# Attention and feed-forward layer on one core: the second layer norm folded into the second weights and the last sum, four tiles sharing a bank for the input transposes and for the output products

## The reference, cut to what matters

```python
def _layernorm(x, eps=1e-5):                      # no gain, no bias
    return (x - mean(x)) / sqrt(var(x) + eps)

x = x + attention(_layernorm(x), Wq, Wk, Wv, Wp, bp)
# attention: q, k, v per head, softmax(q k / 8) v, heads joined, times Wp, plus bp
x = x + ffn(_layernorm(x), ln1_g, ln1_b, w1, b1, ln2_g, ln2_b, w2, b2)

def ffn(x):
    h = layer_norm(x, ln1_g, ln1_b)
    h = einsum('bsd,hd->bsh', h, ternary_quant(w1)) + b1
    h = gelu(h)
    h = layer_norm(h, ln2_g, ln2_b)               # over the 512 hidden columns
    return einsum('bsh,dh->bsd', h, ternary_quant(w2)) + b2
```

## Time and profile before

| | |
|---|---|
| runs | 1081.8, 1083.76, 1084.48 us, median 1083.76 us |
| the profiled execution | 1080.79 us, of which the span of the core's work is 1079.0 us |
| busy share of the span | PE 95%, PE weight loads 74%, DVE 86%, ACT 88%, POOL 85% |
| granted TensorE clock, mean | 0.989 |
| first stage | from the start to about 951 us |
| second stage alone | from about 951 us to the end |

### The profile page before, as it was taken

How to read it: one execution, slowest core, us unless ns; L and a number is a source line. 1 busy time by engine, 2 the same in 40 slices (tenths; PEclk the granted TensorE clock), 3 DMA queues, 4 the chain that set the end, 5 groups by cost and what they waited for, 6 DMA issues and landing times.

```text
span 1079.0 us, 40480 instructions
## 1 busy us (share of the span) xinstructions
PE 1021.4 (95%) x16160; PEld 801.4 (74%) x16160; DVE 923.9 (86%) x1989; ACT 952.3 (88%) x1322; POOL 920.0 (85%) x874
## 2 busy tenths in 40 slices
PE   2878999988999999999999999999999999789998
PEld 1456776766877777778777777777777778567777
DVE  5889888898888888888888888888888888579998
ACT  2677997987999999999999999999999999779997
POOL 3376997987899999999999999999999998967785
PEclk9999999999999999999999999999999999989999
DMA  9201232112222233222322222222222222311111
GB/s 201 68 12 30 42 41 40 36 33 36 42 42 42 41 42 42 41 41 40 35 44 40 40 39 40 39 40 39 42 41 42 41 42 41 61 30 32 41 32 50
DMA packets 159785, 47.56 MB, mean 44 GB/s; under 512 B 141168, under 2 KB 159344, under 8 KB 159600
## 3 DMA queue, kind: packets, MB, share of 16 engines
q1 hardware_dynamic: 159600, 44.97, 23.0%
HBM read 7.21 MB, written 4.19 MB: 11 GB/s over the span
## 4 chain that ended last, share of the span: by engine, by line
PE 74%; ACT 10%; DVE 7%; issue 6%; POOL 2%; DMA 1%; ACTq 0%; SPq 0%; DVEq 0%; POOLq 0%
PE S L471 14%; PE PV L490 7%; PE S L463 7%; PE PV L492 5%; PE PV L491 5%; PE QK L431 5%; PE QK L432 5%; PE QK L433 5%; PE M L444 5%; ACT zTh L750 3%; ACT z L737 3%; PE misc L524 2%; PE misc L504 2%; PE misc L525 2%; PE misc L526 2%
## 5 line engine op out<-in xcount | busy, mean ns | idle before, releaser
L805 POOL TENSOR_TENSOR pl<-p,ph 128x1024 f16<-128x1024 f32 x256 | 545.4, 2136 | 85.0 <-ACT ph L677 80.8
L669 ACT ACTIVATE p<-S,s_exp 128x1024 f32<-128x1024 f32 x256 | 285.3, 1114 | 56.3 <-PE S L471 53.7
L943 DVE TENSOR_REDUCE negmax<-M 128x4 f32<-128x1024 f32 x256 | 311.9, 1218 | 7.4 <-PE M L444 4.0
L677 ACT ACTIVATE ph<-p 128x1024 f16<-128x1024 f32 x256 | 270.6, 1057 | 8.1
L971 DVE TENSOR_TENSOR QKl<-QK,QKh 128x512 f16<-128x512 f32 x256 | 176.3, 689 | 98.7 <-ACT QKh L685 98.5
L490 PEld LDWEIGHTS PV<-V,ph 128*128 128x128 f16 x2048 | 185.3, 98 | 65.9 <-issue 63.9
L490 PE MATMUL PV<-V,ph 128*128 128x65 f16 x2048 | 216.3, 194 | 11.7 <-DVE O L965 11.5
L491 PE MATMUL PV<-V,ph 128*128 128x64 f16 x2048 | 214.2, 193 | 0.0
L492 PE MATMUL PV<-V,pl 128*128 128x65 f16 x2048 | 213.4, 194 | 0.0
L492 PEld LDWEIGHTS PV<-V,pl 128*128 128x128 f16 x2048 | 189.2, 97 | 0.0
L491 PEld LDWEIGHTS PV<-V,ph 128*128 128x128 f16 x2048 | 189.1, 97 | 0.0
(11 more groups left out here) (145 smaller groups left out, 2481.0 us busy)
## 6 DMA issues: line engine op xcount, KB each, us to landing
result<-X SPq DMA_DIRECT2D x16, 256.0 KB, 2.3
X<-in_L_attn_query SPq DMA_DIRECT2D x7, 512.0 KB, 7.1
OT<-O SPq DMA_TRANSPOSE x64, 4.3
O<-in_L_attn_Wq SPq DMA_DIRECT2D x1, 512.0 KB, 4.7
O<-in_L_attn_Wk SPq DMA_DIRECT2D x1, 512.0 KB, 6.5
X<-in_L_attn_query SPq DMA_DIRECT2D x2, 256.0 KB, 5.2
O<-in_L_attn_Wv SPq DMA_DIRECT2D x1, 512.0 KB, 5.9
w<-in_L_ffn_w SPq DMA_DIRECT2D x2, 256.0 KB, 5.0
```

The source lines that it names most:

```text
L669: e.activation(p32[r][:, :, :, :].rearrange("p i m n -> p (i m n)"), S[:, :], ACT.Exp, scale=s_exp[:, :]).then_inc(s_ex, 1)
L677: e.activation(ph[r][:, :, :, :].rearrange("p i m n -> p (i m n)"), p32[r][:, :, :, :].rearrange("p i m n -> p (i m n)"), ACT.Copy).then_i ...
L805: e.tensor_tensor(pl[r][:, :, :, :].rearrange("p i m n -> p (i m n)"), p32[r][:, :, :, :].rearrange("p i m n -> p (i m n)"), ph[r][:, :, : ...
L943: e.tensor_reduce(negmax[g % 2][:, :].rearrange("p (i c) -> p i c", i=2)[:, :, NB * jj:NB * jj + NB], M[:, :].rearrange("p (i t m) -> p i ...
```

## The change

Second layer norm. `z` is no longer made. PE transposes the gelu's output `a` itself. The mean is taken out of the second weights once (a new matmul with `ones` at step `MEAN2` = 56, new DVE instruction `T2_less`), since subtracting from each row of products the mean is the same as using weights whose mean over the 512 hidden rows is gone. The inverse root, times the scale factors `s_f1` and `s_f2`, goes into the last sum as `rs2`. POOL makes it for four tiles at a time. The split of the turned values now also multiplies by `inv_f1` (one number per partition): on ACT a scale operand, on DVE `scalar_tensor_tensor` in place of `tensor_tensor`.

Groups of four (`FG`). The transposes of four tiles' `y` fill one bank, and `yTh` and `yTl` are made with one instruction of 512 columns for four tiles. The products of four tiles fill one `misc` bank, and the sums of a group begin when its fourth product is done. `y` is made by ACT, with `r1` and a new `nm1` that POOL computes with two more instructions per batch. `FFN_LEAD` goes from 2 to 5, and the lags change.

```diff
-FFN_LEAD, TAIL = 2, 7
-QK_RING, P_RING, XT_RING, A_RING = 10, 4, 3, 5
+FFN_LEAD, TAIL = 5, 7
+QK_RING, P_RING, XT_RING, A_RING = 10, 4, 3, 4
+FG = 4
-L_YT, L_YLO, L_HID, L_STAT, L_NORM, L_ZT, L_ZLO, L_OUT, L_SUM = 1, 2, 3, 4, 6, 7, 8, 9, 10
+L_YT, L_HID, L_ZT, L_OUT, L_SUM = 1, 6, 7, 9, 13
-T1_SPLIT, GAINS2, BIAS2 = MAXIMA["t1"][2] + 1, 52, 56
+T1_SPLIT, GAINS2, MEAN2, T2_SPLIT, BIAS2 = MAXIMA["t1"][2] + 1, 52, 56, 58, 64
...
         def f_bank(i):
-            return misc_banks[i % 2]
+            return misc_banks[1 - i // FG % 2]
...
+                if t == MEAN2:
+                    dst = misc_take("mean2", 0)
+                    e.wait_ge(s_w, W_AT["T2"])
+                    for c in range(FC):
+                        op = e.matmul(dst[:, 0:D], ones[:, :], above[1][:, c * D:(c + 1) * D], start=c == 0, stop=c == FC - 1)
+                    op.then_inc(s_fb, 1)
...
             def f_hidden(i):
-                e.wait_ge(s_ylo, i + 1)
+                g, k = divmod(i, FG)
+                e.wait_ge(s_ylo, g + 1)
...
             def f_zT(i):
-                e.wait_ge(s_z, i + 1)
+                e.wait_ge(s_a, i + 1)
...
             def f_out(i):
+                g, k = divmod(i, FG)
                 e.wait_ge(s_zlo, i + 1)
-                if i < 2:
-                    e.wait_ge(*misc_done(*misc_lists[i][-1]))
-                if i >= 2:
-                    e.wait_ge(s_out, i - 1)
-                o = f_bank(i)[:, 0:D]
+                if k == 0 and g < 2:
+                    e.wait_ge(*misc_done(*misc_lists[1 - g][-1]))
+                elif k == 0:
+                    e.wait_ge(s_out, FG * (g - 1))
+                o = f_bank(i)[:, k * D:(k + 1) * D]
...
-            def f_norm(i):
-                k = i % A_RING
-                e.wait_ge(s_nm2, i + 1)
-                if i >= 2:
-                    e.wait_ge(s_zt, i - 1)
-                e.activation(z[i % 2][:, :], a[k][:, :], ACT.Identity, scale=r2[k][:, :], bias=nm2[k][:, :]).then_inc(s_z, 1)
+            def f_y(i):
+                g, k = divmod(i, FG)
+                e.wait_ge(s_nm1, i // NB + 1)
+                if g >= 2:
+                    e.wait_ge(s_yt, FG * (g - 2) + k + 1)
+                e.activation(y[g % 2][:, k, 0:D - 1], X[:, i, 0:D - 1], ACT.Identity, scale=r1[:, i:i + 1],
+                             bias=nm1[:, i:i + 1]).then_inc(s_y1, 1)
...
-                             ACT.Copy).then_inc(s_zhi, 1)
...
+                             ACT.Identity, scale=inv_f1[:, :]).then_inc(s_zhi, 1)
+
+            def f_yhi(g):
+                e.wait_ge(s_yt, FG * g + FG)
+                if g >= 2:
+                    e.wait_ge(s_pre, FG * (g - 1))
+                e.activation(yTh[g % 2][:, :, :], yT_bank[g % 2].rearrange("p (k n) -> p k n", k=FG),
+                             ACT.Copy).then_inc(s_yhi, 1)
...
-                for lag, fn in ((L_NORM, f_norm), (L_HID, f_gelu), (L_ZT, f_zhi), (L_YT, f_yhi)):
+                for lag, fn in ((L_HID, f_gelu), (L_ZT, f_zhi), (0, f_y)):
                     if 0 <= u - lag < NT:
                         fn(u - lag)
+                if u % FG == 0 and FG <= u <= NT:
+                    f_yhi(u // FG - 1)
...
                 e.tensor_tensor(r1[:, tl], ve1[:, tl], half[:, :], ALU.pow).then_inc(s_r1, 1)
+                e.wait_ge(s_r1, b + 1)
+                e.tensor_tensor(mr1[:, tl], mv1[:, tl, 0], r1[:, tl], ALU.mult).then_inc(s_mr1, 1)
+                e.wait_ge(s_mr1, b + 1)
+                e.tensor_scalar(nm1[:, tl], mr1[:, tl], -1.0, None, ALU.mult).then_inc(s_nm1, 1)
...
+            def f_root(g):
+                k = g % 2
+                e.wait_ge(s_mv2, FG * g + FG)
+                e.tensor_scalar(ve2[k][:, :], mv2[k][:, :, 1], EPS, None, ALU.add).then_inc(s_ve2, 1)
+                e.wait_ge(s_ve2, g + 1)
+                e.tensor_tensor(r2[k][:, :], ve2[k][:, :], half[:, 0:1].to_broadcast([P, FG]), ALU.pow).then_inc(s_r2, 1)
+                e.wait_ge(s_r2, g + 1)
+                if g >= 2:
+                    e.wait_ge(s_out, FG * (g - 1))
+                e.tensor_scalar(rs2[k][:, :], r2[k][:, :], s_f12[:, :], None, ALU.mult).then_inc(s_rs2, 1)
...
+                if t == MEAN2:
+                    e.wait_ge(s_fb, 3)
+                    weight(e.scalar_tensor_tensor(above[1][:, :].rearrange("p (c d) -> p c d", c=FC),
+                                                  misc("mean2", 0)[:, 0:D].unsqueeze(1).to_broadcast([P, FC, D]), -1.0 / F,
+                                                  above[1][:, :].rearrange("p (c d) -> p c d", c=FC), ALU.mult, ALU.add),
+                           "T2_less")
...
-                e.tensor_tensor(zTl[i % 3][:, :, :], z_bank[i % 2][:, :].rearrange("p (c n) -> p c n", c=FC),
-                                zTh[i % 3][:, :, :], ALU.subtract).then_inc(s_zlo, 1)
+                e.scalar_tensor_tensor(zTl[i % 3][:, :, :], z_bank[i % 2][:, :].rearrange("p (c n) -> p c n", c=FC),
+                                       inv_f1[:, :], zTh[i % 3][:, :, :], ALU.mult, ALU.subtract).then_inc(s_zlo, 1)
 
             def f_sum(i):
-                e.wait_ge(s_f, i + 1)
+                g, k = divmod(i, FG)
+                e.wait_ge(s_f, FG * g + FG)
                 e.wait_ge(s_xb, i + 1)
-                e.scalar_tensor_tensor(X[:, i, :], f_bank(i)[:, 0:D], s_f2[:, :], X[:, i, :],
+                e.wait_ge(s_rs2, g + 1)
+                e.scalar_tensor_tensor(X[:, i, :], f_bank(i)[:, k * D:(k + 1) * D], rs2[g % 2][:, k:k + 1], X[:, i, :],
                                        ALU.mult, ALU.add).then_inc(s_out, 1)
...
+                if u % FG == 1 and FG < u <= NT + 1:
+                    f_ylo(u // FG - 1)
+                for lag, fn in ((L_ZT, f_stats), (L_SUM, f_sum), (L_ZT, f_variance), (L_ZT, f_zlo)):
```

More of the change, by code:

```diff
@@ L206, in layer @@
         st1, mv1 = sb("st1", [P, NB, 6]), sb("mv1", [P, NT, 2])
-        ve1, r1 = sb("ve1", [P, NT]), sb("r1", [P, NT])
+        ve1, r1, mr1, nm1 = (sb(n, [P, NT]) for n in ("ve1", "r1", "mr1", "nm1"))
         setup = ExitStack()
@@ L233, in layer @@
         setup.close()
-        y = [sb(f"y{i}", [P, D]) for i in range(2)]
-        yTh = [sb(f"yTh{i}", [P, P], F16) for i in range(3)]
-        yTl = [sb(f"yTl{i}", [P, P], F16) for i in range(3)]
+        y = [sb(f"y{i}", [P, FG, D]) for i in range(2)]
+        yTh = [sb(f"yTh{i}", [P, FG, P], F16) for i in range(2)]
+        yTl = [sb(f"yTl{i}", [P, FG, P], F16) for i in range(2)]
         a = [sb(f"a{i}", [P, F]) for i in range(A_RING)]
-        z = [sb(f"z{i}", [P, F]) for i in range(2)]
         zTh = [sb(f"zTh{i}", [P, FC, P], F16) for i in range(3)]
@@ L591, in f_hidden @@
                 o = pre_bank[i % 2]
-                e.matmul(o, yTh[i % 3][:, :], T1h[:, :], start=True, stop=False)
-                e.matmul(o, yTh[i % 3][:, :], T1l[:, :], start=False, stop=False)
-                e.matmul(o, yTl[i % 3][:, :], T1h[:, :], start=False, stop=True).then_inc(s_pre, 1)
+                e.matmul(o, yTh[g % 2][:, k, :], T1h[:, :], start=True, stop=False)
+                e.matmul(o, yTh[g % 2][:, k, :], T1l[:, :], start=False, stop=False)
+                e.matmul(o, yTl[g % 2][:, k, :], T1h[:, :], start=False, stop=True).then_inc(s_pre, 1)
             def f_zT(i):
-                e.wait_ge(s_z, i + 1)
+                e.wait_ge(s_a, i + 1)
                 if i == 0:
@@ L621, in f_yT @@
             def f_yT(i):
+                g, k = divmod(i, FG)
                 e.wait_ge(s_y1, i + 1)
                 if i == 0:
+                    e.wait_ge(s_y0, 2)
                     e.wait_ge(s_mx, NP)
-                if i >= 2:
-                    e.wait_ge(s_ylo, i - 1)
-                e.transpose(yT_bank[i % 2][:, 0:P], y[i % 2][:, :], ident[:, :]).then_inc(s_yt, 1)
+                if k == 0 and g >= 2:
+                    e.wait_ge(s_ylo, g - 1)
+                e.transpose(yT_bank[g % 2][:, k * P:(k + 1) * P], y[g % 2][:, k, :], ident[:, :]).then_inc(s_yt, 1)
             e.wait_ge(s_ident, 2)
@@ L741, in f_gelu @@
                 if i >= A_RING:
-                    e.wait_ge(s_z, i - A_RING + 1)
-                    e.wait_ge(s_mv2, i - A_RING + 1)
-                e.activation(a[i % A_RING][:, :], pre_bank[i % 2][:, :], ACT.Gelu, scale=s_f1[:, :]).then_inc(s_a, 1)
+                    e.wait_ge(s_zt, i - A_RING + 1)
+                    e.wait_ge(s_st2, i - A_RING + 1)
+                e.activation(a[i % A_RING][:, :], pre_bank[i % 2], ACT.Gelu, scale=s_f1[:, :]).then_inc(s_a, 1)
             def f_zhi(i):
@@ L876, in pool_program @@
                     e.wait_ge(s_w, W_AT["ffn_weights"])
-                for lag, fn in ((L_STAT, f_root), (L_STAT, f_negmean), (0, f_bias)):
-                    if 0 <= u - lag < NT:
-                        fn(u - lag)
+                if 0 <= u < NT:
+                    f_bias(u)
+                if (u - L_ZT) % FG == FG - 1 and 0 <= u - L_ZT < NT:
+                    f_root((u - L_ZT) // FG)
```

86 lines of the change are left out of this document (31 added, 55 removed), and 1 row of the table W_AT.

## The result

The changed kernel took 1075.95 us (median of 6 runs, 1074.98 to 1079.46), the kernel before 1083.76 us (6 runs, 1081.8 to 1084.48) in the same comparison. The ratio is 0.9936, interval 0.992 to 0.9952. The profiled execution took 1075.9 us, span 1074.1. So the change is faster, as forecast, but by more than the range allowed (1077.0 to 1084.6).

The account below looks back on a forecast made before the run. The prediction took PE to bound attention and DVE, at 1.96 us a tile, the second stage. Its terms -4.25, -2.35, +2.0 and +1.25 sum to -3.35 us; against the median of 1083.76 it forecast 1080.4 us, range 1077.0 to 1084.6.

Parts of the forecast that it names:

- 60 tiles: Second stage, tile 3 to tile 63: PE becomes the bound at 1.87 us a tile, -4.25 us (bounds -5.5 and -2.5).
- from the last hidden values to the end: End of the kernel: the root leaves the path, 9.35 us instead of 11.7, -2.35 us (bounds -3.3 and -1.2).
- a term of the attention part that was put at nothing: Middle of attention: POOL's new 0.68 us a batch lies in its 1.3 us of idle time, so no cost.
- POOL at the end of attention: Three more bias additions and three longer roots on POOL, less tile 0's root: +2.0 us (bounds +1.1 and +3.6).
- The prediction's sign: End of attention: POOL's last `O` starts about 2 us later than 941.76, plus what attention lost.
- The weights: Attention stage: the mean's matmuls take 1.1 us on PE, `T2_less` can delay PE: +1.25 us (bounds +0.5 and +2.8).
- The stall of step 56 only moves to step 64: Weights term, attention stage: moving the last weight step shifts its stall; no separate cost was given.
- The second step that failed: Final sum: the median of the runs lies 3 us above the profiled execution, so 1077.4 became 1080.4 us.
- PE at 1.87 us a tile as the new bound: Second stage: DVE and ACT fall to 1.75 us a tile, under PE's 1.87, which becomes the bound.
- The rival of the group hand-over: Second stage: the 0.1 us slack becomes a wait of about 0.3 us a group; 1084.3 us, no change; chance 0.15.
- The rival of the slow `zTl`: Second stage: the new `zTl` takes long and DVE sets the stage; gain gone, or up to 1108 us; chance 0.05.
- The rival "more gain": Attention: the weights' matmuls hide and POOL's chain isn't lengthened, giving 1077.2 us; chance 0.12.

Follow-up runs that it names:

- the pair: Kernel before and changed kernel, both with `lbrep1` two steps earlier, second-weight pieces one a step, early tiles' bias additions late, last weight step at 64: 1070.24 and 1066.1 us.
- the partner: Kernel before with `lbrep1` two steps earlier, second-weight pieces one a step, bias additions of tiles 0 to 5 late, last weight step at 64: 1070.24 us, ratio 0.9877.
- the combined kernel: Changed kernel with `lbrep1` two steps earlier, second-weight pieces one a step, bias additions of tiles 0 to 8 late: 1066.1 us, ratio 0.9842.
- its repeat: The kernel before, unchanged, run and profiled a second time: 1083.52 us, ratio 1.0003, span 1083.7.

## Why the prediction was wrong

The terms, in us: as forecast; as the two profiles have them; and in the pair of kernels without the large single waits (spans 1068.4 and 1064.2). For the pair the hidden values of tile 3 and the line with its last start are, in the partner and in the combined kernel:

```profile
940.10 0.38 PE L593 MATMUL S<-T1h,yTh 128*128 128x512 f16 x1
...
L593 PE MATMUL S<-T1h,yTh x64: 377/389/390, 925.5 to 1056.7; 128*128 128x512 f16 x64
```

```profile
942.40 0.38 PE L604 MATMUL S<-T1h,yTh 128*128 128x512 f16 x1
...
L604 PE MATMUL S<-T1h,yTh x64: 377/379/390, 927.5 to 1054.5; 128*128 128x512 f16 x64
```

| | forecast | changed minus before | combined minus partner |
|---|---|---|---|
| up to the hidden values of tile 3 (weights, POOL) | +3.25 | +1.1 | +2.3 |
| 60 tiles | -4.25 | -3.9 | -4.5 |
| from the last hidden values to the end | -2.35 | -2.1 | -2.0 |
| sum | -3.35 | -4.9 | -4.2 |

**The step that failed** is a term of the attention part that was put at nothing. The prediction costed `mr` and `nm` only at the end of attention, and of the other 29 batches it said that the new 0.68 us "lies in its 1.3 us of idle time". POOL's idle time did absorb them: from step 70 to step 239 the two traces stay within 0.1 us of each other. But at step 32 the two instructions stand ahead of `pl` and changed who came first, and that gave 3.3 us: 1.8 of a wait and 1.4 of the lower clock behind it. So the stretch up to the hidden values of tile 3, forecast at +3.25, measured +1.1. The prediction named POOL's lock as a danger for `zTl` and didn't ask which DVE instruction it already held. `lbrep1` at 2100 ns was in the trace, where the nearest instruction of its size, L951 with its input in PSUM, takes 281.

The two terms that the prediction did have came out fair. *POOL at the end of attention*, forecast +2.0: from step 239 to the hidden values of tile 3 the changed kernel takes 1.8 us more than before. The prediction's sign was a last `O` about 2 us later; counted from step 239 it is 1.5. A root costs 0.45 more, not 0.68: in the rows of step 32 the next instruction starts 1.28 us after the root (164.01 to 165.29) instead of 0.83 (162.59 to 163.42); three of them cost 1.6 us where they were tried alone. In the pair, whose additions are out of the way, the stretch from step 239 to tile 3 still loses 1.15 us (from +1.15 to +2.30); what of it is the roots and what ACT's `y` isn't separated, and POOL's last `O` waits 0.37 us for ACT there. *The weights*, forecast +1.25: from step 50 to step 70 the changed kernel loses 1.3 us on before. The matmuls of the mean took 1.11 us on PE, as forecast:

```profile
252.64 1.11 PE L558 MATMUL misc<-above,ones 128*128 128x128 f32 x8
```

In the pair it is 0.9 us at the step of these matmuls and 1.3 from step 50 to step 70. In the changed kernel the agreement is in part luck. "The stall of step 56 only moves to step 64" was right as to the wait, 3.0 us in both places, but what the clock adds differs from one execution to the next. The windows behind the wait of step 64, in the changed kernel and in the changed kernel without the low product, whose program is the same there:

```profile
283.00:289.00 6.00, 5.01 (x58) 4.21 (x59) 3.47 (x8) 1.34 (x2) 2.68 (x4) 0.72 0.37 69
283.00:289.00 6.00, 6.00 (x106) 4.64 (x105) 4.19 (x8) 4.19 (x5) 3.33 (x3) 1.00 0.48 90
```

At 0.72 the exponential of step 65 comes 8.97 us behind that of step 64, at 1.00 7.51. With the second execution the weights' term would have been -0.2 instead of +1.3.

**The second step that failed** is the last one, adding 3 us for the distance of the median from the profiled execution. It is no constant of the measurement. The profiled execution of before was a quick one: it started early and kept its full clock after the wait of step 52, where its repeat started 1.3 us later and fell to 0.56. The profiled execution of the changed kernel started late and lies at its median. So of the 4.45 us by which the forecast was too high, this addition is 3.0. The other 1.5 is the difference of the sums, -3.35 and -4.9: -3.3 at step 33, +1.4 from a later start (step 16 at 107.18, against 105.75), and +0.4 in everything else.

How often the changed kernel falls to half clock at step 54 isn't shown; it has the same wait of 3.0 us there, and its profiled execution kept the full clock. One of its six runs, 1079.46 with a mean clock of 0.985, looks like an execution that didn't, but only the profiled one has a trace.

**What was right.** Faster was right, but of the 7.8 us between the medians only some 4 are the change; for that part the sum of the four terms, -3.35 us, was close to the pair's -4.2. PE at 1.87 us a tile as the new bound with DVE under it, both shown by leaving out the low product. The rival of the group hand-over is refuted: PE didn't wait once at `yTl` between 960 and 1060 us. The rival of the slow `zTl` is refuted too: none of its 64 took more than 0.752 us, against 0.746 in the earlier trace rows. The slow row there, T1l with its two inputs in SBUF, took between 0.90 and 2.06 us in the runs of this study. The rival "more gain", 1077.2 us, gave a reason that didn't hold (POOL's chain was lengthened), though its number was near.

## What to carry to other kernels

An instruction that takes eight times what its like takes, and ends together with a long one of another engine, has probably waited for it. Look for such rows in the trace before you cost a change, because a small instruction put in ahead of the long one can undo or create the wait, as it did here. To judge what a change is itself worth, take such single waits out of both kernels and compare again; here the answer went from 7.8 to 4.1 us. Where one engine's long preparation makes PE wait, look at the clock behind the wait too: here a wait of 3.0 us cost up to 2.7 us more, and cutting the preparations in pieces, one a step, took 5.4 us off the kernel before and most of its spread. Don't put two sorts of pieces in the same step without trying it: the kernel that did was 4.8 us slower than the one that didn't.
